# First slots of a mixture of experts: token buffers, transposes and one softmax's logits moved ahead

## What is computed

```python
xg = (l2norm(x) * scale * gamma_in)            # x: the layer-normed tokens, in groups of 64
phi = l2norm(slots1) * scale                   # 8 x 16 slots
logits1 = einsum('bGgd,esd->bGges', xg, phi)
disp1 = softmax(logits1, axis=2)               # over the 64 tokens of a group
comb1 = softmax(logits1.reshape(b, G, g, 128), -1)   # over the 128 slots
slots = einsum('bGgd,bGges->bGesd', xg, disp1)
yn = l2norm(slots) * scale * gamma2
means = yn.reshape(b, G, 8, 4, 4, d).mean(axis=4)
```

## Time and profile before

| what | value |
|---|---|
| time, median of 3 runs | 562.56 us (562.29 to 566.72) |
| the profiled execution | 566.14 us, of it 564.4 us span |
| TensorE, busy share of the span | 93% |
| VectorE, ScalarE, GpSimd | 56%, 46%, 15% |
| granted clock of TensorE, mean | 0.985 of full speed |
| first slots, from TensorE's first to VectorE's last instruction | 272.2 to 334.9 us |

### The profile page before, as it was taken

How to read it: one execution, slowest core, us unless ns; L and a number is a source line. 1 busy time by engine, 2 the same in 40 slices (tenths; PEclk the granted TensorE clock), 3 DMA queues, 4 the chain that set the end, 5 groups by cost and what they waited for, 6 DMA issues and landing times. The chain is left out here.

```text
span 564.4 us, 13527 instructions
## 1 busy us (share of the span) xinstructions
PE 525.0 (93%) x5431; PEld 429.5 (76%) x5431; DVE 313.8 (56%) x738; ACT 257.1 (46%) x822; POOL 83.5 (15%) x128
## 2 busy tenths in 40 slices
PE   6999999999999999999777779899989999999997
PEld 5888888766566566667655545688869999999986
DVE  2348778767776786652235755566634344444443
ACT  1234344366656665644345737667643232232320
POOL 6480000011104304400243100001000000000000
PEclk9999999999999999999968999999989999999999
DMA  6180000000000000000600006011129989999833
GB/s 238 40 289 2 2 0 2 1 2 1 1 2 3 1 1 1 2 2 1 235 4 1 1 2 209 1 57 59 61 102 407 423 318 328 302 328 313 250 53 120
DMA packets 20721, 58.79 MB, mean 104 GB/s; under 512 B 3042, under 2 KB 9796, under 8 KB 20548
## 3 DMA queue, kind: packets, MB, share of 16 engines
q1 hardware_dynamic: 14756, 49.47, 24.4%
q0 software_dynamic: 1056, 4.33, 4.1%
q10 hardware_dynamic: 4848, 4.13, 2.5%
HBM read 53.21 MB, written 4.33 MB: 102 GB/s over the span
## 5 line engine op out<-in xcount | busy, mean ns | idle before, releaser
L2095 PE MATMUL banks<-slots_t,w 64*128 64x128 f32 x1536 | 91.4, 272 | 1.1 <-PEq L1806 1.1
L2095 PEld LDWEIGHTS banks<-slots_t,w 64*128 64x128 f32 x1536 | 90.0, 188 | 1.7 <-issue 1.4
L1138 DVE TENSOR_REDUCE qk<-banks 128x4 f32<-128x1024 f32 x48 | 58.8, 1226 | 39.5 <-PE banks L601 39.5
L2168 ACT ACTIVATE ex_gelu<-banks,b_sb 128x128 f32<-128x128 f32 x128 | 36.6, 369 | 90.2 <-PE banks L2095 90.2
L601 PE MATMUL banks<-qk_t 16*128 16x256 f32 x384 | 54.4, 400 | 2.6 <-DVE qk L1138 2.4
L608 PE MATMUL banks<-qk_t 17*128 17x256 f32 x384 | 54.4, 400 | 0.0
L2188 DVE SCALAR_TENSOR_TENSOR ex_act_t<-banks,b_sb,ex_gelu 128x128 f32<-128x128 f32 x128 | 36.1, 344 | 28.9 <-ACT ex_gelu L2168 28.9
L601 PEld LDWEIGHTS banks<-qk_t 16*128 16x128 f32 x384 | 33.2, 184 | 20.3 <-issue 13.8
L2126 PE MATMUL banks<-w,ex_act_t 64*128 64x192 f32 x512 | 47.1, 323 | 1.2 <-DVE ex_act_t L2188 1.2
L2198 DVE TENSOR_REDUCE ex_rows<-banks 128x192 f32<-128x384 f32 x32 | 17.9, 558 | 47.5 <-PE banks L2126 47.5
L2126 PEld LDWEIGHTS banks<-w,ex_act_t 64*128 64x128 f32 x512 | 41.0, 187 | 1.4 <-issue 1.4
(11 more groups left out here) (231 smaller groups left out, 1048.2 us busy)
## 6 DMA issues: line engine op xcount, KB each, us to landing
w<-in_w SPq DMA_DIRECT2D x32, 768.0 KB, 9.9
w<-in_w2e SPq DMA_DIRECT2D x32, 384.0 KB, 10.9
w_slot<-in_w_slot SPq DMA_DIRECT2D x8, 576.0 KB, 3.8
rows_scratch<-ex_rows ACTq DMA_DIRECT2D x28, 96.0 KB, 7.3
yn_all<-rows_scratch POOLq DMA_DIRECT2D x7, 384.0 KB, 9.8
out<-h SPq DMA_DIRECT2D x8, 192.0 KB, 1.9
qkv_w_sb<-in_qkv_w SPq DMA_DIRECT2D x1, 864.0 KB, 5.1
wk_t<-in_wk_t ACTq DMA_DIRECT2D x2, 289.5 KB, 3.4
```

Of the source, the lines that this page charges most:

```text
L1138: nc.vector.tensor_reduce(to, flat(MAXES[0], MAXES[1] + 1).rearrange("p (h t n) -> p h t n", h=2, n=SEQ), AX.X, ALU.max, negate=True).then ...
L2095: return nc.tensor.matmul(bank[:, j * P:(j + 1) * P], g.w1[n % BUFS][rows, first + j * P:first + (j + 1) * P], x, start=start, stop=stop, ...
L2168: nc.scalar.activation(gelu[n % 2][:, j * P:(j + 1) * P], gate_bank(n)[:, j * P:(j + 1) * P], ACT.Gelu_apprx_tanh, bias=g.t["b1"][:, n, HB ...
```

## The change

- Each of the 8 sequences has token buffers of its own (four of them in the memory of the four experts' second layers), and its own `x_t` (in the memory of two experts' first layers).
- POOL makes the tokens of sequences 0 to 6 during attention. Only `make_x(7)` stays in first slots, at the head of POOL's queue.
- The tokens of 0 to 6 are transposed in attention's last body and behind it, by `tokens_last`, and copied by ACT (`keep_tokens`). Four `warm` fillers of the last body and three products behind it fall away. Sequence 7 is turned in step 1 of first slots, through bank MEANS.
- `logits` and `maxima` run one sequence ahead: both of 0 before the loop, of n+1 in step n.
- PE's order of a step: make_slots(n-1), logits(n+1), turn_comb(n-1), turn_disp(n), turn_means(n-3), make_means(n-2). DVE's: maxima(n+1), keep_comb(n-1), norm_slots(n-1), keep_disp(n), keep_means(n-3), invert(n). ACT's is as before without `keep(n+2)`.
- The four second-layer loads wait for make_slots(4) to make_slots(7), each.

```diff
-                if n >= 4:
-                    make_tokens(n - 4)
+                if n >= 3:
+                    make_tokens(n - 3)
+            for n in range(BATCH - 3, MADE_AHEAD):
+                make_tokens(n)
...
+            def tokens_last(n, members):
+
+                if n == BATCH - 1:
+                    for m in members:
+                        pe.wait_ge(g.tokens_made, m + 1)
+                        if m >= 2:
+                            pe.wait_ge(g.x_kept, m - 1)
+                        turn_tokens(nc, g, m, FRONT[m % 2])
...
                 if prev:
                     project(n - 1)
-                warm(n, 3, 0)
+                warm(n, 3)
+                tokens_last(n, (4,))
                 scores_and_maxima((n, 1, 1), nxt(2))
...
-                warm(n, 0, 4)
+                tokens_last(n, (5,))
                 turn_max(n, 2)
...
-            turn(0)
-            keep_busy(nc, g, 6, 3)
-            turn(1)
+            logits(0)
             for n in range(BATCH + 3):
+                if 0 <= n - 1 < BATCH:
+                    make_slots(n - 1)
+                if n + 1 < BATCH:
+                    logits(n + 1)
+                if n == 1:
+                    turn_last_tokens()
+                if 0 <= n - 1 < BATCH:
+                    turn_comb(n - 1)
                 if n < BATCH:
-                    logits(n)
-                if n + 2 < BATCH:
-                    turn(n + 2)
+                    turn_disp(n)
+                if n == BATCH + 1:
+                    turn_rows(2)
                 if 0 <= n - 3 < BATCH:
                     turn_means(n - 3)
-                if 0 <= n - 1 < BATCH:
-                    make_slots(n - 1)
-                if 0 <= n - 1 < BATCH:
-                    turn_comb(n - 1)
-                if n == BATCH + 1:
-                    turn_rows(2)
                 if 0 <= n - 2 < BATCH:
                     make_means(n - 2)
-                if n < BATCH:
-                    turn_disp(n)
...
+            maxima(0)
             for n in range(BATCH + 3):
+                if n + 1 < BATCH:
+                    maxima(n + 1)
+                if 0 <= n - 1 < BATCH:
+                    keep_comb(n - 1)
+                    norm_slots(n - 1)
                 if n < BATCH:
-                    maxima(n)
+                    keep_disp(n)
                 if 0 <= n - 3 < BATCH:
                     keep_means(n - 3)
-                if 0 <= n - 1 < BATCH:
-                    keep_comb(n - 1)
-                if n < BATCH:
-                    keep_disp(n)
-                if 0 <= n - 1 < BATCH:
-                    norm_slots(n - 1)
                 if n < BATCH:
                     invert(n)
...
+            g.clear_before(sp)
             for n in range(EARLY):
+                sp.wait_ge(S["slots_made"], NX + n + 1)
                 load_second_layer(sp, g, n)
-            g.clear_before(sp)
...
+            for n in range(MADE_AHEAD, BATCH):
+                make_x(n)
             for n in range(BATCH):
-                if n + NX < BATCH:
-                    make_x(n + NX)
                 scale_comb(n)
```

More of the change, by code:

```diff
@@ L96, in keep_busy, with turn_tokens, keep_tokens @@
         nc.tensor.matmul(g.ps[bank][:, 0:P], g.ident[:, :], g.ident[:, :], start=True, stop=True)
+def turn_tokens(nc, g, n, bank):
+    for c in range(3):
+        last = nc.tensor.transpose(g.ps[bank][:, c * P:(c + 1) * P], g.tokens[n][:, 1 + c * P:1 + (c + 1) * P],
+                                   g.ident[:, :])
+    last.then_inc(g.x_turned, 1)
+def keep_tokens(nc, act, g, n, bank):
+    act.wait_ge(g.x_turned, n + 1)
+    nc.scalar.copy(g.x_t[n][:, :, :], g.ps[bank][:, 0:3 * P].rearrange("p (c n) -> p c n", c=3)
+                   ).then_inc(g.x_kept, 1)
 def mixer_and_attention(nc, g):
@@ L317, in _ @@
                 nc.gpsimd.memset(x[:, (t + 1) * DIM - 1:(t + 1) * DIM], 1.0).then_inc(S["ones_set"], 1)
-            for s in range(NX):
+            for s in range(BATCH):
                 for col in (0, TPS * (DIM + 1) - 1):
@@ L708, in body @@
                     make_v(n + 1)
-                warm(n, 3, 2)
+                warm(n, 3)
+                tokens_last(n, (2,))
                 scores_and_maxima((n, 0, 1), nxt(1))
@@ L714, in body @@
                     turn_mixed(n - 1)
-                warm(n, 2, 2)
+                warm(n, 2)
+                tokens_last(n, (3,))
                 turn_max(n, 1)
@@ L763, in _ @@
             turn_mixed(BATCH - 1)
-            keep_busy(nc, g, 0, 3)
+            tokens_last(BATCH - 1, (6,))
             project(BATCH - 1)
@@ L944, in body @@
                         root_out(n - 2)
+                    if not fill:
+                        keep_tokens(nc, act, g, 0, FRONT[0])
                     expo(n - 1, 2, 1)
+                if not fill:
+                    keep_tokens(nc, act, g, 1, FRONT[1])
                 if fill:
@@ L956, in body @@
                 expo(n, 0, 1)
+                if not fill:
+                    keep_tokens(nc, act, g, 2, FRONT[0])
                 if n == 0:
@@ L964, in body @@
                 expo(n, 1, 0)
+                if not fill:
+                    keep_tokens(nc, act, g, 3, FRONT[1])
                 if fill:
@@ L969, in body @@
                     keep_fill(n + 1, 2)
+                if not fill:
+                    keep_tokens(nc, act, g, 4, FRONT[0])
                 if stat:
@@ L1338, in _, with turn_last_tokens @@
         def _(pe):
[L1339 to L1349, removed]
+            def turn_last_tokens():
+                pe.wait_ge(S["weighted"], BATCH - MADE_AHEAD)
+                turn_tokens(nc, g, BATCH - 1, MEANS)
             def logits(n):
-                pe.wait_ge(S["kept"], n + 1)
+                pe.wait_ge(g.x_kept, n + 1)
                 if n >= 2:
@@ L2241, in tower @@
         g.w2 = [sb(f"w2_{b}", [P, HID // P, DIM]) for b in range(EARLY)]
+        g.tokens += [g.w2[b][:, :, :].rearrange("p a d -> p (a d)")[:, 0:TPS * (DIM + 1)] for b in range(EARLY)]
         g.w1_loaded = [sem(f"w1_loaded{b}") for b in range(BUFS)]
@@ L2250, in tower @@
                   for n in range(BATCH)]
+        g.x_t = [g.w1[2 + n // 4][:, (n % 4) * 3 * P:(n % 4 + 1) * 3 * P].rearrange("p (c n) -> p c n", c=3)
+                 for n in range(BATCH)]
+        g.tokens_made, g.x_turned, g.x_kept = sem("tokens_made"), sem("x_turned"), sem("x_kept")
         g.yn_turned, g.yn_kept_s, g.yn_kept_v = sem("yn_turned"), sem("yn_kept_s"), sem("yn_kept_v")
```

53 lines of the change are left out of this document (22 added, 31 removed).

## The result

The changed kernel takes 585.66 us (median of 4 runs, 580.87 to 590.23); the kernel before, run beside it, 562.93 (4 runs, 562.29 to 566.72). The ratio is 1.034, with a 95% interval of 1.029 to 1.039: slower, on the side that was forecast, but by about 19 to 23 us where 11.6 were predicted, and above the range. The profiled execution took 590.23 us, its span is 588.5 us against 564.4. So places are read from both.

The account below looks back on a forecast made before the run. The prediction held first slots bound by POOL's order and the clock its gaps cost. New step order +4.2, clock +7 and attention +0.4 made +11.6 us: 562.6 to 574, own range 570 to 578, 8 in 10 from 565 to 582.

Parts of the forecast that it names:

- The ring: First slots: queue waits from one make_means through logits, norm_slots and keep_means to the next, 7.29 us a step at high clock.
- PE's longest waits: Sign in first slots: PE waits longest at make_means, released by DVE's means_t copies.
- the clock's term: First slots: 3.5 of six steps from make_slots(1) to (7) run at the low clock, +7 us.
- the tail: End of first slots after make_slots(7): 5.28 us to make_means(6), then 8.05; low clock at most 2 more, none taken.
- The sum at the high clock: Whole of first slots, its steps added up without clock loss: 66.9 us against 62.7, +4.2.
- a slow step: First slots: a step with logits and slots or means at the low clock costs 2.0 us more.
- the clock is low throughout: Rival for first slots: every step at the low clock, +18.6 us in all, 581 us; chance 0.20.
- my estimate by it, 10.5: First slots: half of 42 us throttled, by the skill's rule, costs 10.5 us instead of 7, making 578 us.
- attention, +0.4: Attention's last body: only tokens_last(4) adds time, +0.4 us; transposes in place of fillers change nothing.
- a stage after first slots that changes by over a microsecond: Sign that the prediction is wrong: a stage after first slots changes by more than a microsecond.
- The rival of 554 us: Rival for first slots: make_means never waits for keep_means, steps of 5.64 us, 554 us; chance 0.08.

Follow-up runs that it names:

- e8_after: The changed kernel run again unaltered, in the same call as later experiments: 585.88 us.
- e3_double: The changed kernel with three more VectorE copies ahead of keep_means, into a tile nobody reads: 591.7 us.
- e2_fill: The changed kernel with products of the identity put back into attention's last body: 580.33 us.
- e9: The changed kernel with eight more products of the identity at the end of first slots: 583.43 us.
- e10: e1_old_order with eight more products of the identity at the end of first slots: 558.32 us.
- e11: e4_all with two in place of ten filler products at attention's end: 558.15 us.
- e7_first: e4_all with logits and maxima one sequence ahead and make_slots first in TensorE's step: 576.14 us.
- e4_all: The changed kernel with the old step order in first slots and the products put back in attention's last body: 553.82 us.
- e5_unfill: The kernel before without the three products ahead of turn_max(7, 0) in attention's last body: 566.84 us, ratio 1.000.
- e1_old_order: The changed kernel with the old order of steps in first slots put back on TensorE and VectorE: 560.33 us.

## Why the prediction was right and wrong

**The ring: right, to its parts.** Predicted 7.29 us at the high clock; the turn above took 8.40. VectorE's part, maxima to the next means, was predicted as 0.70 + 0.40 + 1.30 + 0.40 + 1.07 = 3.87, measured 0.67 + 0.33 + 1.30 + 0.33 + 1.08 = 3.71. The rest, with TensorE in it, was predicted as 0.60 + 1.07 + 1.75 = 3.42 and measured as 0.92 + 1.46 + 2.31 = 4.69: means, slots and logits at 1.2 GHz. PE's longest waits are where they were predicted, the wait of turn_comb for POOL shrank to 1.6 us, and the tokens, ACT's copies and the late second-layer loads cost nothing that the traces show.

**The step that failed: the clock's term.** "I take 3.5 of six, +7." By step, predicted at the high clock and measured: 4.65 and 4.7; 7.24 and 7.20; 5.64 and 7.64; 7.08 and 9.37; 7.29 and 8.07; 7.29 and 9.03; 7.29 and 8.05; 7.10 and 7.26; the tail 13.33 and 15.5. The sum at the high clock was 66.9; the stage took 76.9, and 77.7 in e8_after. That sum stands up where it can be checked: the step to make_slots(2), at 1.2 GHz throughout in the changed kernel, took 7.64, which is 5.64 and the 2.0 that I had put on a slow step, and e3_double's step at the full clock took 7.48 where 7.08 + 0.59 was to be expected. So the clock costs 10.0 and 10.8, not 7. The steps have 7.7 of it (8.5 in e8_after): that this is near my 7 is partly luck, since I had 3.5 slow steps at 2.0 each, and five had 0.8 to 2.3 and the last 0.2. The mis-sized part is the tail, for which I took nothing in the sum although I had named 2 as its bound: it lost 2.2. The low clock was not over after part of the steps but came back in all of them, down to the tail. The rival "the clock is low throughout", with 14 for it, overstates it by 3 to 4 us.

The Trainium skill ("TensorE: Matmul & The Clock Gate", Terms) puts the penalty at the throttled time times one minus the clock ratio; my estimate by it, 10.5, came close to what was measured, but by luck. It assumed 21 us of throttled time. The stage and the stretch of low clock in attention's last body:

```profile
277.82:354.67 76.85, 52.05 (x339) 37.58 (x339) 32.07 (x100) 30.82 (x157) 7.89 (x11) 0.73 0.13 44
244.50:258.20 13.70, 13.32 (x92) 8.11 (x96) 4.97 (x7) 4.85 (x9) 1.64 (x2) 0.50 0.00 1
```

A mean of 0.73 between the two levels is some 41 us at 1.2 GHz in the stage. By the rule they would cost about 20 us; they cost 10.0. TensorE is busy for only 52 of the stage's 77 us, and its waits for other engines are there at either clock. Where it is busy nearly throughout, in attention, the rule gives 6.9 us, and the trace is nearer to it: first slots starts 5.1 us later than in e8_after, the same kernel without the fall (277.82 against 272.71).

**The step that failed first: attention, +0.4.** "Where transposes take the place of fillers, nothing changes" was not so. Three of the products that went, those ahead of `turn_max(7, 0)`, have nothing in their place, and five ahead of the scores, 1.38 us, became six transposes of 0.87 us; I had not laid fillers and transposes side by side: five `warm` calls of the last body go, with 5, 3, 2, 2 and 4 products, not four as "The change" says, and one of the five is replaced by nothing. PE then stands 0.60 and 0.82 us, the clock falls in most executions, and attention ends 5.2 us later than I wrote. In e8_after, where it did not fall, the term held: 0.5 us. That the cost depends on the execution fits the changed kernel's runs, which spread over 9 us with a whole-kernel clock of 0.971 in the shortest and 0.948 in the longest, against 2 us in e2_fill's; where the clock fell is known only of the executions traced.

**A term in none of the cases: the experts, 1.7 to 2.3 us over the 129.4 of before.** I named a stage after first slots that changes by over a microsecond as a sign that I am wrong, and it was. The cause is not any work of the change, but the place of the experts' code in TensorE's stream: 32 instructions put in ahead of it end the loss (e9 and e10), 32 taken out bring it on (e11). In the profiled execution the last mix adds 2.6 us, with a clock that fell in it (7.10 us for 64 products in place of 5.42); e8_after has 5.42 there, so that is not the change's.

**What no run decides.** The rival of 554 us takes keep_means out of the ring. e7_first does not test that: it moves keep_means ahead of norm_slots, the ring closes through it all the same, and the kernel takes 576.1. What e7_first shows is that the old order's early keep_means, worth 4.2 us there, leaves the ring closed once make_slots stands first. The rival's own step of 5.64 us, make_slots, logits, maxima and norm, agrees with the one step that has no keep_means (7.64 with 2.0 for the clock, above). The gain that the rival promised exists, but in e4_all, with the order untouched.

The sum as measured, with e8_after: stage 15.0, start of first slots 0.5, later stages 2.6: 18.1 of span; in the profiled execution 14.2 + 5.6 + 4.3 = 24.1. Predicted were 11.2 + 0.4 + 0.

## What to carry to other kernels

Buffers that free an engine's queue and an order that moves work ahead are two changes: here the first, with its fillers kept, is worth -11 us (e4_all) and the second +27 (e2_fill over e4_all), and only kernels with one of them alone showed it. Before work is moved ahead in a queue, follow every wait of the moved instruction through the queues of all engines back to itself; a step can't be shorter than the longest such ring, and moving one link ahead in its queue may leave the ring closed, as in e7_first. Price a clock that may fall over every step and the tail of a stage whose steps all have gaps, and lay removed fillers one by one beside what replaces them.

## What the runs showed of the hardware

- The clock fell from 2.4 to 1.2 GHz around gaps of 0.60 and 0.82 us of TensorE, in a stretch in which it was busy 7.2 to 7.7 of 8.5 us (236 to 244.5), in five executions of six, and stayed low for 7, 10, 10, 14 and 34 us. With seven products of the identity back between 240 and 260 us, five of them ahead of 245.2, it never fell in five executions (8.14 of 8.5 us busy in e2_fill and e4_all).
- A gap of 0.82 us alone (e5_unfill) did not make it fall; a wait of 1.96 us ahead of first slots (e11_shift) came with a first step at 0.53.
- Some 41 us at 1.2 GHz cost 10.0 us, against a sum of rows at the full clock, in a stage where TensorE is busy 52 of 77 us; 13.7 us at 1.2 GHz cost 5.1, against another execution of the same kernel, where it is busy 13.3 of them.
- The same experts' code takes 129.2 or 131.1 to 132.1 us. Within two pairs of kernels (e1_old_order and e10_pad_old, e4_all and e11_shift) it goes with nothing but 32 instructions of TensorE ahead of it, through three or four stops, three of them at the same blocks each time. What TensorE stands for in them no run shows.
